# One step of a dense graph attention: the score products move from behind the transposes to the end of the step

## The chip, the core and the metric

The kernel runs on one core of one Trainium2 chip, as one launch. TensorE (PE) does the products and the transposes, VectorE (DVE) and ScalarE (ACT) the elementwise work, GpSimd (POOL) small parts, and SyncE (SP) issues most of the transfers. The metric is the device time of one execution in microseconds (us). Three timed runs of the kernel before gave 3488.07, 3489.20 and 3493.47 us, median 3489.2 us.

## The reference, cut to what matters

Four graph layers follow one another on 3125 nodes, 256 features and 100,000 edges, each with a residual and a layer norm behind it. The change touches only the first, an attention with 4 heads of 64 features:

```python
q = jnp.einsum('nd,hdk->nhk', x, Wq) + bq
k = jnp.einsum('nd,hdk->nhk', x, Wk) + bk
v = jnp.einsum('nd,hdk->nhk', x, Wv) + bv
scores = jnp.sum(q[dst] * k[src], axis=-1) / np.sqrt(HEAD_DIM).astype(np.float32)
seg_max = jax.ops.segment_max(scores, dst, num_segments=N)
ex = jnp.exp(scores - seg_max[dst])
denom = jax.ops.segment_sum(ex, dst, num_segments=N)
alpha = ex / (denom[dst] + 1e-16)
agg = jax.ops.segment_sum(alpha[:, :, None] * v[src], dst, num_segments=N)
out_h = agg + jnp.einsum('nd,hdk->nhk', x, Wskip) + bskip
```

The kernel does it densely. It counts the edges of every pair of nodes once, and each attention is then a softmax over a whole row of 3200 source nodes (25 tiles of 128), with the logarithm of the edge count added to the score; pairs without an edge get a huge negative number.

## The kernel before, in words

**The parts of the program.** They run one after the other: the edge counts and the projections, the first attention (names a_p_s, a_p_t, a_p_o; about 542 to 1580 us of the profile), the second attention by the same function `attend` with `dot=False` (to about 2470 us), and the sums with the last attention.

**The unit.** The first attention goes through 25 tiles of 128 target nodes times 4 heads, 100 units. A unit passes through these steps:

1. Scores (`score_part`, L1132): the 128 x 3200 scores are made in 8 pieces of 400 columns, each of two matmuls with the full 128 x 128 array (from sh_kt and sh_q) into one of two banks a_p_s. DVE adds the masks, takes the maximum and so frees the bank (`masked`, L1305; semaphore s_sfree), two pieces per slot.
2. ACT takes the exponential in place in a_sm (L1214; s_prob).
3. Transposes (`turn_block`, L1150): PE transposes the 25 blocks of a_sm in four slots of 7, 7, 7 and 4 blocks (`DOT_TURNS`, L805) into the two banks a_p_t, and ACT copies each slot back into a_sm (L1220; s_copy).
4. Weighing (`weigh`, L1173): 25 matmuls of the values a_v (64 columns) with the transposed rows. Block a writes partitions 0 to 63 or 64 to 127 of a_p_o, by whether a is even or odd (`r = (a % 2) * HD`), and the 25 blocks add up there. The profile shows each of these matmuls as two instructions, so 7 blocks are x14.
5. ACT copies the sums into a_sumT (`flip`, L1227; s_flip), PE turns them back (`turn_back`, L1180), and ACT scales them (L1239).

**The order.** It is written out by hand, engine by engine. In the loop step of unit n, PE transposes unit n, weighs unit n-1, makes the scores of unit n+2 and turns back unit n-2, slot by slot (u = 0 to 3). The steps for the layer's output (`posts`, names a_pp) come at the end of slots 1 and 3. With T, W and S for the transposes, the weighing and the scores of a slot, the order of the first attention is T0 S0 W0, W1 T1 S1, T2 S2 W2, W3 T3 S3, turn back. In the second attention there are no scores, and the order is T0 W0, T1 W1, T2 W2, T3 W3, with 8, 8, 8 and 1 blocks.

**The waits around it on PE.** A score piece waits until the piece two before it is masked, and the first score piece of a tile for its loads. T of a slot waits for the exponential of its columns and for the copy of the transposes two slots before. W0 waits for the flip of unit n-2, which ACT does at the start of the same step, behind the scaling of that unit; that scaling waits for the turn back at the end of the step before.

Of the kernel before, what the change touches and what calls it, by code (L numbers as in the profile page):

```python
# [808 lines left out]
def attend(nc, name, ident, dot, heads, passes, v_dram, post, full_dram, shared, log_dram=None, q_dram=None, kt_dram=None, al_src_dram=None, al_dst_dram=None, ct_dram=None, r2_dram=None):  # L809

    ctx = ExitStack()
    with ctx:
# [63 lines left out]
        def loaded(j):  # L876

            return 144 * (j // 2) + (128 if j % 2 else 0)
# [6 lines left out]
        def unit(p, j, par, half, h):  # L885

            t, gp, gh = tile_of(p, j, par, half)
            return t * heads + h, h if heads == 4 else 2 * gp + h

        def exists(at):  # L890

            return at is not None and not (isinstance(at[1], int) and at[1] >= NT)

        def following(at):

            p, j, par, half, h = at
            if h + 1 < heads:
                return p, j, par, half, h + 1
            if isinstance(j, int) and j == NT - 1 and p < final:
                return p + 1, 0, 0, 0, 0  # L900
            return p, j + 1, 1 - par, (half + 1 if par == 1 else half), 0
# [10 lines left out]
        def ahead(at, k):  # L912
            for _ in range(k):
                at = following(at)
            return at if exists(at) else None

        def behind(at, k):
            for _ in range(k):
                at = preceding(at) if at is not None else None
            return at if exists(at) else None  # L920
# [9 lines left out]
        def early(n, k):  # L930
            return isinstance(n, int) and n < k

        def units_loop(eng, body):

            for p in range(passes):
                tile_run(lambda j, par, half, first=False, last=False: [body((p, j, par, half, h)) for h in range(heads)])
            for k in range(P_.LAGS):
                for h in range(heads):
                    body((final, NT + k, (NT + k) % 2, (NT + k) // 2, h))

        def posts(eng, fn, at, u):

            p, j, par, half, h = at
            if p == final:
                for step in lagged(j, par, half):
                    fn(eng, h * ntu + u, *step)

        def score_bank(n, i):

            if n >= len(first_units):  # L950
                return p_s[i % 2][:, 0:SW]
            pair = (n * SU + i) // 2 % RING
            o = (i % 2) * UNIT
            return p_s[i % 2][:, 0:SW] if pair == 0 else p_t[pair - 1][:, o:o + SW]
# [4 lines left out]
        with nc.Block() as block:  # L959
# [154 lines left out]
            @block.tensor  # L1114
            def _(pe):
                def score_part(at, k, m):

                    p, j, par, half, h = at
                    n, buf = unit(*at)
                    if k == 0 and m == 0:  # L1120
                        if n == 0:
                            pe.wait_ge(shared.s_q, 128)
                        elif h == 0:
                            pe.wait_ge(s_in[par], loaded(j))
                        if n < heads:
                            pe.wait_ge(shared.s_kt[h], 96 if h < 2 else 32)
                    r, l = divmod(m, 2)
                    i = 2 * k + r
                    freed = n * SU + i - (1 if n >= len(first_units) else 2 * RING - 1)
                    if l == 0 and freed >= 1:  # L1130
                        pe.wait_ge(s_sfree, freed)
                    t = nc.tensor.matmul(score_bank(n, i), q[par][:, h, l, :], shared.keys(h)[:, i * SW:(i + 1) * SW], start=l == 0, stop=l == 1)  # L1132
                    if l == 1:
                        t.then_inc(s_s, 1)

                def turn_block(at, u, i):

                    n, buf = unit(*at)
                    if i == 0:
                        if u == 0 or e_part[u] != e_part[u - 1]:  # L1140
                            pe.wait_ge(s_prob, n * NE + e_part[u] + 1)
                        if dot and n == 0 and u == 0:
                            pe.wait_ge(s_sfree, len(first_units) * SU)
                        done = n * ntu + u - 1
                        if not early(done, 1):
                            pe.wait_ge(s_copy, done)
                        if u == 1 and not early(n, 3):
                            pe.wait_ge(s_norm, n - 2)
                    a = a_row[u] + i
                    m = nc.tensor.transpose(p_t[u % 2][:, i * P:(i + 1) * P], sm[buf][:, a * P:(a + 1) * P], ident[:, :])  # L1150
                    if i == turns[u] - 1:
                        m.then_inc(s_t, 1)

                def turn_and_score(at, u):

                    later = ahead(at, 2) if dot else None
                    for i in range(turns[u] if exists(at) else 0):
                        turn_block(at, u, i)
                    for m in range(0 if later is None else SCORE_PARTS):
                        score_part(later, u, m)  # L1160

                def weigh(at, u):

                    n, buf = unit(*at)
                    p, h = at[0], at[4]
                    if u == 0 and not early(n, 1):
                        pe.wait_ge(s_flip, n)
                    if early(n, 1) and u == 0:
                        pe.wait_ge(s_v, 16 if dot else 48)
                    pe.wait_ge(s_copy, n * ntu + u + 1)  # L1170
                    for a in range(a_row[u], a_row[u + 1]):
                        r = (a % 2) * HD
                        m = nc.tensor.matmul(p_o[r:r + HD, 0:P], v[:, a, (p * heads + h) * HD:(p * heads + h + 1) * HD], sm[buf][:, a * P:(a + 1) * P],  # L1173
                                             start=a < 2, stop=a >= NT - 2)
                    m.then_inc(s_pv, 1)

                def turn_back(at):
                    n, buf = unit(*at)
                    pe.wait_ge(s_flip, n + 1)
                    nc.tensor.matmul(back, sumT[:, at[4] % 2, :], twice[:, :], start=True, stop=True).then_inc(s_back, 1)  # L1180

                def body(at):
                    for u in range(ntu):
                        turns_first = not dot or u % 2 == 0
                        if turns_first:
                            turn_and_score(at, u)
                        if behind(at, 1) is not None:
                            weigh(behind(at, 1), u)
                        if not turns_first:
                            turn_and_score(at, u)  # L1190
                        if u == back_slot and behind(at, 2) is not None:
                            turn_back(behind(at, 2))
                        posts(pe, P_.pe, at, u)
                    if not dot and at[0] == 0 and at[4] == 0:
                        P_.pe_heavy(pe, at[1])
                    if isinstance(at[1], int) and at == first_tile_end:
                        P_.pe_init(pe)

                pe.wait_ge(s_const, 3)
                if dot:  # L1200
                    for at in first_units:
                        for k in range(SU // 2):
                            for m in range(SCORE_PARTS):
                                score_part(at, k, m)
                units_loop(pe, body)

            @block.scalar
# [196 lines left out]
SCORE_PARTS = 4  # L1404
# [600 lines left out]
class Tail:  # L2005
# [314 lines left out]
    def turn(self, pe, j, u):  # L2320

        if u == 0 or self.e_part[u] != self.e_part[u - 1]:
            pe.wait_ge(self.s_prob, j * NE + self.e_part[u] + 1)
        n = j * len(TURNS) + u
        if n >= 2:
            pe.wait_ge(self.s_copy, n - 1)
        for i in range(TURNS[u]):
            a = self.a_row[u] + i
            m = self.nc.tensor.transpose(self.p_t[u % 2][:, i * P:(i + 1) * P], self.sm[j % 2][:, a * P:(a + 1) * P], self.ident[:, :])  # L2329
        m.then_inc(self.s_t, 1)  # L2330
# [341 lines left out]
```

## Time and profile before

| what | value |
| --- | --- |
| timed runs, median of 3 | 3489.2 us |
| profiled execution, whole time | 3502.71 us |
| its span | 3501.0 us |
| PE busy | 3303.7 us (94%) |
| DVE busy | 2600.1 us (74%) |
| ACT busy | 2083.2 us (60%) |
| mean granted clock of TensorE | 0.984 of 2.4 GHz |

The profile is one execution. Busy time is time in which at least one instruction of an engine was under way; matmuls overlap, so the mean duration of one (some 280 ns for a 128-column matmul) says less than the distance from one to the next. A timeline row merges the instructions of one line: its first number is the start, the second its length, then the engine, the line, the operation, the output and inputs, and after x how many there are. In square brackets stands how long the engine had been idle just before and what ended that.

### The profile page before, as it was taken

What the parts mean: (1) busy time and instruction counts of PE and PEld (TensorE: products, weight loads), DVE (VectorE), ACT (ScalarE), POOL (GpSimd) and SP (SyncE); (2) the same over time, 40 slices, a digit from 0 to 9 for tenths busy, and PEclk for the clock granted to TensorE, in tenths of its full rate; (3) what the DMA queues carried; (4) which work ended last, traced back from release to release, by engine and by line L of the source; (5) the groups of instructions that cost most, each with busy time, mean ns of one, the idle gap of its engine ahead of it and who ended that gap; (6) DMA issues with size and microseconds to landing.
All of it is one profiled execution on the core that took longest, in us unless ns stands there. A gap on an engine that the chain in (4) does not pass through costs nothing. (4 is left out here: it accounts for less than half of the span.)

```text
span 3501.0 us, 67240 instructions
## 1 busy us (share of the span) xinstructions
PE 3303.7 (94%) x25814; PEld 2685.9 (77%) x25815; DVE 2600.1 (74%) x4799; ACT 2083.2 (60%) x3840; POOL 647.3 (18%) x604
## 2 busy tenths in 40 slices
PE   5999997999999999997999999999899999999998
PEld 3555556888888888885777777777688888878887
DVE  7899986766766766658999999999698443235665
ACT  2556555777766766776999999999211111115554
POOL 1010000111111111111255146666100000000000
PEclk9999998999999999998999999999999999999999
DMA  2565667333333433346333523333665555553341
GB/s 75 229 235 208 238 236 215 103 118 120 107 106 114 125 107 105 111 142 160 104 116 118 193 92 132 106 132 102 226 221 208 210 204 192 217 208 129 136 148 58
DMA packets 202699, 534.72 MB, mean 153 GB/s; under 512 B 56881, under 2 KB 165462, under 8 KB 168502
## 3 DMA queue, kind: packets, MB, share of 16 engines
q1 hardware_dynamic: 199494, 526.25, 43.5%
q10 hardware_dynamic: 1904, 3.81, 0.4%
q8 instruction: 191, 3.13, 0.4%
q0 software_dynamic: 1024, 0.82, 0.1%
q14 instruction: 86, 0.70, 0.1%
HBM read 362.87 MB, written 167.80 MB: 152 GB/s over the span
## 5 line engine op out<-in xcount | busy, mean ns | idle before, releaser
L1220 ACT ACTIVATE a_sm<-a_p_t 128x896 f32<-128x896 f32 (+3 forms) x800 | 670.5, 838 | 292.6 <-PE a_p_t L1150 235.3
L1150 PE MATMUL a_p_t<-ident,a_sm 128*128 128x128 f32 x5000 | 709.8, 279 | 34.7 <-ACT a_sm L1220 20.2
L1214 ACT ACTIVATE a_sm<-a_sm,a_negm 128x896 f32<-128x896 f32 (+3 forms) x600 | 702.7, 1171 | 48.5 <-DVE a_negm L1277 48.1
L1173 PE MATMUL a_p_o<-a_sm,a_v 128*64 128x128 f32 x10000 | 706.0, 280 | 21.4 <-ACT a_sumT L1227 19.2
L1173 PEld LDWEIGHTS a_p_o<-a_sm,a_v 128*64 128x64 f32 x10000 | 560.8, 138 | 142.5 <-issue 88.2
L1150 PEld LDWEIGHTS a_p_t<-ident,a_sm 128*128 128x128 f32 x5000 | 558.1, 142 | 135.0 <-issue 115.4
L1305 DVE CUSTOM_DVE_ANT_0 a_sm<-a_p_s,sh_rows 128x400 f32<-128x400 f32 x790 | 421.9, 571 | 308.5 <-PE a_p_s L1132 267.4
L1132 PE MATMUL a_p_s<-sh_kt,sh_q 128*128 128x400 f32 x1580 | 395.4, 371 | 36.5 <-DVE a_mx L1305 17.5
L1326 DVE SCALAR_TENSOR_TENSOR a_sm<-sh_wide,sh_al 128x3125 f32<-128x3125 f32 x100 | 346.9, 3469 | 3.6 <-PEq L54 1.8
L1336 DVE CUSTOM_DVE_ANT_0 a_sm<-a_sm,sh_rows 128x3125 f32<-128x3125 f32 x100 | 348.1, 3481 | 1.3 <-issue 0.3
L1132 PEld LDWEIGHTS a_p_s<-sh_kt,sh_q 128*128 128x128 f32 x1580 | 263.0, 191 | 49.8 <-DVE a_mx L1305 27.0
L2344 PE MATMUL t_acc<-t_v,t_sm 128*128 128x256 f32 x1250 | 287.5, 381 | 0.0
L583 DVE TENSOR_TENSOR hot_k<-iota_w,key_g 128x2400 bf16<-128x2400 f16 x200 | 279.7, 1399 | 0.0
L738 ACT ACTIVATE sh_wide<-p_g 128x400 f32<-128x400 f32 x200 | 149.3, 904 | 207.4 <-PE p_g L653 207.4
L2344 PEld LDWEIGHTS t_acc<-t_v,t_sm 128*128 128x128 f32 x1250 | 230.4, 191 | 31.9
L651 PE MATMUL p_g<-hot_k,hot_b 128*128 128x400 bf16 x1200 | 228.7, 340 | 21.0 <-DVE hot_k L583 20.3
L2228 PE MATMUL t_acc<-sh_messages,sh_ct 128*128 128x512 f32 x825 | 221.9, 410 | 9.9 <-PEq L54 9.2
L651 PEld LDWEIGHTS p_g<-hot_k,hot_b 128*128 128x128 bf16 x1200 | 113.7, 98 | 120.9 <-DVE hot_k L583 37.0
L2375 ACT ACTIVATE t_hT<-t_pp 128x256 f32<-128x256 f32 x50 | 19.3, 385 | 279.5 <-PE t_pp L2280 279.5
L2228 PEld LDWEIGHTS t_acc<-sh_messages,sh_ct 128*128 128x128 f32 x825 | 152.3, 190 | 39.9 <-issue 9.6
L2405 ACT ACTIVATE t_sm<-t_p_t 128x1024 f32<-128x1024 f32 x100 | 83.5, 835 | 165.3 <-PE t_p_t L2329 165.3
L2184 POOL TENSOR_SCALAR t_n_ve<-t_n_mv 128x1 f32<-128x1 f32 x50 | 10.9, 219 | 739.1 <-DVE t_n_mv L2583 531.8
(319 smaller groups left out, 4859.8 us busy)
## 6 DMA issues: line engine op xcount, KB each, us to landing
sh_rows<-d_full SPq DMA_DIRECT2D x67, 1600.0 KB, 7.1
sh_ct<-d_ct SPq DMA_DIRECT2D x50, 1600.0 KB, 6.7
d_ct<-sh_wide SPq DMA_DIRECT2D x25, 1600.0 KB, 5.3
d_full<-sh_rows SPq DMA_DIRECT2D x25, 1600.0 KB, 5.9
t_third<-d_ct SPq DMA_DIRECT2D x25, 1600.0 KB, 6.7
d_logs<-sh_rows SPq DMA_DIRECT2D x23, 1664.0 KB, 6.0
sh_rows<-d_logs SPq DMA_DIRECT2D x23, 1664.0 KB
sh_q<-d_q SPq DMA_DIRECT2D x200, 64.0 KB, 2.3
```

The source lines that it names most:

```text
L583: v.tensor_tensor(hot_k[k][:, q, :, :, :], iota_w[:, :, :].unsqueeze(1).to_broadcast([P, TRIP // 2, GW, 2]), by_two(key_g[k][:, q, :], GW) ...
L651: last = nc.tensor.matmul(p_g[:, q, 0:GW], hot_b[k][:, q, u // 2, :, u % 2], hot_k[k][:, q, u // 2, :, u % 2], start=False, stop=u == TRIP ...
L1132: t = nc.tensor.matmul(score_bank(n, i), q[par][:, h, l, :], shared.keys(h)[:, i * SW:(i + 1) * SW], start=l == 0, stop=l == 1)
L1150: m = nc.tensor.transpose(p_t[u % 2][:, i * P:(i + 1) * P], sm[buf][:, a * P:(a + 1) * P], ident[:, :])
L1173: m = nc.tensor.matmul(p_o[r:r + HD, 0:P], v[:, a, (p * heads + h) * HD:(p * heads + h + 1) * HD], sm[buf][:, a * P:(a + 1) * P], start=a ...
L1214: nc.scalar.activation(sm[buf][:, c], sm[buf][:, c], ACT.Exp, bias=negm[:, buf:buf + 1], accum_out=parts[:, buf, e:e + 1]).then_inc(s_prob, 1)
L1220: nc.scalar.activation(sm[buf][:, a_row[u] * P:a_row[u + 1] * P], p_t[u % 2][:, 0:turns[u] * P], ACT.Copy).then_inc(s_copy, 1)
L1305: v_.tensor_tensor_reduce(out=sm[buf][:, c], in0=score_bank(n, i), in1=full[par][:, c], scale=1.0, scalar=-3.0e38, op0=ALU.add, op1=ALU.ma ...
L1326: v_.scalar_tensor_tensor(sm[buf][:, 0:N], a_bc[:, h, 0, 0:N], al[gp][:, g:g + 1], a_bc[:, h, 1, 0:N], ALU.add, ALU.max).then_inc(s_lift, 1)
L1336: v_.tensor_tensor_reduce(out=sm[buf][:, 0:N], in0=sm[buf][:, 0:N], in1=mask[gp][:, 0:N], scale=1.0, scalar=-3.0e38, op0=ALU.add, op1=ALU. ...
L2228: m = self.nc.tensor.matmul(self.acc[t % 2][:, :], self.ct[t % 3][:, a * P:(a + 1) * P], self.messages[k % 2][:, a, :], start=a == 0, stop ...
L2344: m = self.nc.tensor.matmul(self.acc[t % 2][:, 0:D], self.sm[j % 2][:, a * P:(a + 1) * P], self.v3[:, a, :], start=a == 0, stop=a == NT - 1)
```

## The change

In each slot the scores of unit n+2 are made last, after both the transposes and the weighing. Nothing changes in slots 1 and 3, where they were last already. In slots 0 and 2 the order goes from T S W to T W S. Only PE's order changes, and only in the first attention. Every instruction, every buffer and every wait is as before.

```diff
-                def turn_and_score(at, u):
+                def score_ahead(at, u):
 
                     later = ahead(at, 2) if dot else None
+                    for m in range(0 if later is None else SCORE_PARTS):
+                        score_part(later, u, m)
+
+                def turn(at, u):
+
                     for i in range(turns[u] if exists(at) else 0):
                         turn_block(at, u, i)
-                    for m in range(0 if later is None else SCORE_PARTS):
-                        score_part(later, u, m)
...
                         turns_first = not dot or u % 2 == 0
                         if turns_first:
-                            turn_and_score(at, u)
+                            turn(at, u)
                         if behind(at, 1) is not None:
                             weigh(behind(at, 1), u)
                         if not turns_first:
-                            turn_and_score(at, u)
+                            turn(at, u)
+                        score_ahead(at, u)
                         if u == back_slot and behind(at, 2) is not None:
                             turn_back(behind(at, 2))
```

PE's queue in one unit of the first attention, from T0 to S1, before. The transposes (L1150) are followed by the scores (L1132), and W0 and W1 (L1173) stand together as 14 blocks:

```order
L1150 MATMUL a_p_t<-ident,a_sm 128x128 x7
L1132 MATMUL a_p_s<-sh_kt,sh_q 128x400 x4
L1173 MATMUL a_p_o<-a_sm,a_v 64x128 x14
L1150 MATMUL a_p_t<-ident,a_sm 128x128 x7
L1132 MATMUL a_p_s<-sh_kt,sh_q 128x400 x4
```

The same place of the changed kernel, where the weighing is L1176:

```order
L1150 MATMUL a_p_t<-ident,a_sm 128x128 x7
L1176 MATMUL a_p_o<-a_sm,a_v 64x128 x7
L1132 MATMUL a_p_s<-sh_kt,sh_q 128x400 x4
L1176 MATMUL a_p_o<-a_sm,a_v 64x128 x7
L1150 MATMUL a_p_t<-ident,a_sm 128x128 x7
L1132 MATMUL a_p_s<-sh_kt,sh_q 128x400 x4
```

The one run of 14 blocks has become two of 7, with the scores between them.

PE's queue from T2 to S3 before, where W2 and W3 stand together as 11 blocks:

```order
L1150 MATMUL a_p_t<-ident,a_sm 128x128 x7
L1132 MATMUL a_p_s<-sh_kt,sh_q 128x400 x4
L1173 MATMUL a_p_o<-a_sm,a_v 64x128 x11
L1150 MATMUL a_p_t<-ident,a_sm 128x128 x4
L1132 MATMUL a_p_s<-sh_kt,sh_q 128x400 x4
```

The same place of the changed kernel:

```order
L1150 MATMUL a_p_t<-ident,a_sm 128x128 x7
L1176 MATMUL a_p_o<-a_sm,a_v 64x128 x7
L1132 MATMUL a_p_s<-sh_kt,sh_q 128x400 x4
L1176 MATMUL a_p_o<-a_sm,a_v 64x128 x4
L1150 MATMUL a_p_t<-ident,a_sm 128x128 x4
L1132 MATMUL a_p_s<-sh_kt,sh_q 128x400 x4
```

Here the run of 11 has become one of 7 and one of 4. In the whole program PE's queue grows from 3398 such rows to 3592, two more in each of 97 units: the first unit has nothing to weigh, and the last two make no scores.

## Rows read from the trace of the kernel before

**Rows 1.** Windows: length, then busy us (count) of PE, PEld, DVE, ACT, POOL; PEclk, DMA share, GB/s.
```profile
570.00:1560.00 990.00, 967.13 (x9291) 858.23 (x9289) 679.36 (x2194) 718.07 (x1294) 137.16 (x208) 0.99 0.36 113
```

**Rows 2.** Groups by line, 560 to 1560 us: busy us, mean ns, idle before by releaser.
```profile
L1132 PE MATMUL a_p_s<-sh_kt,sh_q 128*128 128x400 f32 x1555 | 388.1, 371 | 22.2 <-DVE a_mx L1305 16.9 <-DMA sh_kt<-d_kt 5.3
...
L1173 PE MATMUL a_p_o<-a_sm,a_v 128*64 128x128 f32 x4866 | 324.7, 280 | 5.3 <-ACT a_sumT L1227 3.2 <-issue 2.1
```

**Rows 3.** Waits, 560 to 1560 us: total us, times, longest.
```profile
PE a_p_s L1132 <- DVE a_mx L1305: 16.9, 10, 3.2
...
PE a_p_o L1173 <- ACT a_sumT L1227: 3.2, 12, 0.3
```

**Rows 4.** Timeline of PE, first attention, W2 and W3 up to S1 of the next unit.
```profile
621.40 1.52 PE L1173 MATMUL a_p_o<-a_sm,a_v 128*64 128x128 f32 x22
622.86 0.65 PE L1150 MATMUL a_p_t<-ident,a_sm 128*128 128x128 f32 x4
623.27 0.98 PE L1132 MATMUL a_p_s<-sh_kt,sh_q 128*128 128x400 f32 x4
624.08 0.33 PE L1180 MATMUL a_p_t<-a_twice,a_sumT 128*128 128x64 f32 x2
624.25 0.94 PE L1150 MATMUL a_p_t<-ident,a_sm 128*128 128x128 f32 x7
624.94 0.98 PE L1132 MATMUL a_p_s<-sh_kt,sh_q 128*128 128x400 f32 x4
625.85 1.75 PE L1173 MATMUL a_p_o<-a_sm,a_v 128*64 128x128 f32 x28
627.53 0.98 PE L1150 MATMUL a_p_t<-ident,a_sm 128*128 128x128 f32 x7
628.27 0.98 PE L1132 MATMUL a_p_s<-sh_kt,sh_q 128*128 128x400 f32 x4
```

**Rows 5.** Timeline of PE, second attention, W3 of one block up to T1.
```profile
1999.98 0.43 PE L1173 MATMUL a_p_o<-a_sm,a_v 128*64 128x128 f32 x2
2000.34 0.43 PE L1180 MATMUL a_p_t<-a_twice,a_sumT 128*128 128x64 f32 x2
2000.61 1.04 PE L1150 MATMUL a_p_t<-ident,a_sm 128*128 128x128 f32 x8
2001.58 1.09 PE L1173 MATMUL a_p_o<-a_sm,a_v 128*64 128x128 f32 x16
2002.61 1.10 PE L1150 MATMUL a_p_t<-ident,a_sm 128*128 128x128 f32 x8
```

**Rows 6.** Timeline of all engines, PE's weight loads (PEld) into and out of a weighing.
```profile
1004.63 1.28 PEld L1173 LDWEIGHTS a_p_o<-a_sm,a_v 128*64 128x64 f32 x22 [0.27 <-issue]
...
1006.08 0.42 PEld L1150 LDWEIGHTS a_p_t<-ident,a_sm 128*128 128x128 f32 x4 [0.17 <-issue]
```

**Rows 7.** Timeline of PE, two of the ten waits for the masking, and what follows.
```profile
982.65 1.70 PE L1132 MATMUL a_p_s<-sh_kt,sh_q 128*128 128x400 f32 x4 [3.20 <-DVE a_mx L1305]
984.28 2.20 PE L1173 MATMUL a_p_o<-a_sm,a_v 128*64 128x128 f32 x22
...
1484.88 0.64 PE L1132 MATMUL a_p_s<-sh_kt,sh_q 128*128 128x400 f32 x2 [1.85 <-DVE a_mx L1305]
1485.44 1.52 PE L1173 MATMUL a_p_o<-a_sm,a_v 128*64 128x128 f32 x22
```

**Rows 8.** Timelines of ACT and PE: a usual flip, then a late one.
```profile
1007.95 0.27 ACT L1227 ACTIVATE a_sumT<-a_p_o 128x128 f32<-128x128 f32 x1
...
1007.48 0.94 PE L1150 MATMUL a_p_t<-ident,a_sm 128*128 128x128 f32 x7
...
705.23 0.32 ACT L1227 ACTIVATE a_sumT<-a_p_o 128x128 f32<-128x128 f32 x1
...
703.67 0.93 PE L1150 MATMUL a_p_t<-ident,a_sm 128*128 128x128 f32 x7
...
705.60 1.75 PE L1173 MATMUL a_p_o<-a_sm,a_v 128*64 128x128 f32 x28 [0.27 <-ACT a_sumT L1227]
```

## The prediction, made before the changed kernel was run

> **What bounds the kernel now.** I read the profile from the stage down to single products. First the windows: from 570 to 1560 us, nearly all of the first attention, PE is busy for 967 of 990 us at a granted clock of 0.99, while DVE is busy for 679 and ACT for 718 [rows 1]. So PE sets the time there, and what the change adds to PE's own sequence lands on the span, since the next stage begins when this one is done. Then the groups and the waits: all that PE loses to others in this stretch is 16.9 us of score products waiting for DVE's masking, 10 times, 3.2 us of weighing waiting for ACT's flip, 12 times, and 5.3 us once for a load of the keys [rows 2, 3]. A better order of the same instructions has at most these some 25 us to win. Last the timeline of one quiet unit, which shows what PE's sequence costs without any wait, from the start of one block to the start of the next [rows 4]: 7 transposes 0.69 us after the turn back and 0.74 after a weighing, scores 0.81 before the turn back and 0.91 before a weighing, a weighing of 14 blocks (x28) 1.68, one of 11 blocks (x22) 1.46.
>
> **What a run of weighing costs.** This decides the case. Even and odd blocks go to different halves of the array. If the two halves work side by side, one pair of blocks (four instructions) is two passes of time, and a block without a partner takes two passes as well. The rows say so. 14 blocks are 7 pairs, 14 passes: 1.68 us. 11 blocks are 5 pairs and one alone, 12 passes: 1.46 us. The difference of 0.22 for two passes is 0.11 per pass, and it leaves 1.68 - 14 x 0.11 = 0.14, with the unrounded pass of 0.109 some 0.15 per run, whatever its length. In the second attention 8 blocks are 8 passes, which gives 1.02 and reads 1.03, and a single block is 2 passes, 0.37, and reads 0.36 [rows 5]. A rule of one pass per block without the rounding up would give the single block 0.26 and the 11 blocks 1.35, which the rows refuse. Beside the 0.15 per run there is the way in: scores take 0.91 before a weighing and 0.81 before a full-width product [rows 4], 0.10 more. In both places PE's weight loads stand still for no other engine, 0.27 us on the way in and 0.17 on the way out [rows 6].
>
> **The change, first place (T0 to T1).** Before: T0 0.69 + S0 0.91 + W0 and W1 1.68 = 3.28 us [rows 4]. After, T0 leads into a weighing: the second attention shows 8 transposes after a turn back into a weighing at 0.97 [rows 5], and one transpose is (0.74 - 0.41) / 3 = 0.11 [rows 4], so 0.86. W0 has 7 blocks, 3 pairs and one alone, 8 passes like the run of 8: 1.03. S0 now begins in an array that has just left a weighing. No row shows scores behind a weighing. From below it is the 0.91 of scores behind transposes. From above it is 0.96, since transposes lose 0.05 there (0.74 against 0.69). The nearest row is a half of scores that began after a wait: 0.56 us to the weighing [rows 7], where half of the usual four products, (0.91 - 0.18) / 2 + 0.18 by their spacing of 0.18 us (0.91 for four and one more spacing), makes 0.545, so 0.015 more. I take 0.93. W1 has 7 blocks, again 8 passes: 1.03. Sum 0.86 + 1.03 + 0.93 + 1.03 = 3.85, so +0.57 us.
>
> **Second place (T2 to T3).** Before: 0.69 + 0.91 + 1.46 = 3.06. After: T2 0.86, W2 of 7 blocks 1.03, S2 0.93, W3 of 4 blocks, 4 passes, 0.15 + 4 x 0.11 = 0.59. Sum 3.41, so +0.35 us. There is no added lone block here, because 11 blocks had one already.
>
> Together 0.92 us per unit, of which 0.22 is the lone block of the first place and the rest four more changes between half and full width. Times 97 units: **+89 us**. The eight rounded terms may be off by 0.04 us a unit, 4 us in all.
>
> **What hides it.** Nothing that I find: no other engine is near its bound in this stage, and a unit only becomes longer, so DVE, ACT and the loads get more time, not less.
>
> **Waits that change.** (a) W0 loses the cover of S0 while it waits for the flip. In the usual unit the flip ends at 1007.95 + 0.27 = 1008.22, and with T0 at 1007.48 the weighing could now begin at 1007.48 + 0.86 = 1008.34; a flip reaches it some 0.05 us after its end (705.55 to 705.60) [rows 8]. That leaves 0.07 us, which is enough but thin. In the late case the flip ends at 705.55, and T0 began at 703.67, so W0 could begin at 704.53 and waits until 705.60, about 1.07 us, where it waits about 0.3 now. For 12 such units [rows 3] that is at most 12 x 0.75 = +9 us. But between T2 and T3 ACT now has 0.35 us more to catch up, so I take **+5 us**. Below: 0. (b) The scores' waits for the masking [rows 3]. The large ones stand in front of S2 or in its middle, where DVE has been held up itself. The run W2 can now be done within the wait, up to 1.02 us of each. Taken over the ten this is about 7 us, and after a wait of 3.20 us the granted clock was at 1.2 GHz for a while, the x22 run lasting 2.20 instead of 1.52 [rows 7]; a shorter wait may save one or two of these. Also the second score run no longer follows the first so closely (S1 to S2 gains W2's time). I take **-9 us**; from above 0, from below all 16.9 and some 5 of clock, -22.
>
> Sum: 89 + 5 - 9 = +85 us. The profiled execution, 3502.7 us whole (its span is 3501.0), becomes 3588. It lies 13.5 us above the median of the runs; the timed median goes from 3489.2 to **3574 us**, 2.4% slower.
>
> The Trainium skill, in TensorEngine Tiling (Array Packing), Key Properties, says that "Changing tiling mode (not just tile) drains the TensorE"; it gives no price. The 0.15 per run and the idle weight loads of rows 6 agree with it. It is the rule that speaks against this change, since it makes each of the four new changes of width cost something, W to S too.
>
> **The rivals.**
> 1. *Scores follow a weighing for free.* The run's 0.15 is read only where transposes or the turn back follow it; if the scores' products could be loaded behind a weighing as they are behind transposes, 2 x 0.15 and 2 x 0.02 per unit fall away, 0.34 x 97 = 33 us: +52, 3541 us. Against it: transposes too are full width, and their loads stand idle for 0.17 [rows 6]. The Trainium skill, TensorE: Matmul & The Clock Gate, on the engine's queue depths, has a reorder window that pulls weight loads ahead of running matmuls; by it alone this rival would be right, and rows 6 shows that the window does not reach over a change of width. Chance 0.13.
> 2. *The flip's cover goes everywhere.* The margin of 0.07 us is gone if ACT is a little later in the usual unit, as when a copy of 0.6 us comes before the scaling. If half of the 97 units then wait 0.5 us: +24, 3598 us. For it: the 12 late units, and that the second attention, which has this order, waits for the same flip. Against it: units with a post product between turn back and T0 have 0.2 us more. Chance 0.10.
> 3. *Faster, because the masking is what holds PE.* With the scores at even distances, DVE never holds a bank, the 16.9 us and the slow clock behind them go (-22), and the mode changes cost nothing, because the half-width passes are only the spacing of a busy queue: 3467 us. It wins over the cost only if a unit grows by less than 22 / 97 = 0.23 us. The single block of rows 5, 0.36 us for one product, alone speaks against it. Chance 0.03.
> 4. *No change*: the added time lies where PE would have waited anyway. PE's idle time of about 23 us in 990 [rows 1] has no room for 89. Chance 0.02.
> 5. *The lone block is not paid* (it overlaps the scores' first load): 0.22 x 97 = 21 us less, 3553 us. Against it: 11 blocks, with a lone last one, pay their 12th pass before transposes. Chance 0.10.
>
> The forecast of 3574 has the remaining 0.62. A measurement of this kernel can tell about 0.2%, 7 us, from no change; faster than that 0.03, within it 0.02, slower 0.95. The range goes from 3535 us (rival 1 with all that the waits could give beyond the 9 taken for a part of it) to 3600 us (rival 2).
>
> **What the profile of the changed kernel would show.** From T0 to T1 of a quiet unit 3.85 us, from T2 to T3 3.41, with W0, W1 and W2 each as x14 and 1.03 us to the next block, and W3 as x8 and 0.59. The first attention ends about 85 us later, and the second attention has its old length. Weight loads of the scores idle for about 0.2 us behind each weighing; if they don't, it is rival 1. The flip's waits remain about 12 but near 1 us, and many more would be rival 2. Score waits for the masking drop below 10 us. The forecast is wrong if T0 to T1 takes under 3.5 us, or if PE's idle time in this stage grows by more than 20 us.

## The result, and the profile after

| | before | changed |
| --- | --- | --- |
| timed runs, median | 3491.3 us (4 runs) | 3564.4 us (4 runs, 3560.6 to 3567.1) |
| profiled execution, whole | 3502.7 us | 3562.8 us |
| its span | 3501.0 us | 3561.1 us |

The changed kernel is slower by 73 us: ratio 1.0198, interval 1.0179 to 1.0217. The forecast was +85 us, to 3574 us with a range of 3535 to 3600.

The place first. The view of one line's instructions gives, for each kind, the count, the shortest, median and longest duration in ns, and the start of the first and the last one in us. The score products of before, then of the changed kernel:

```profile
L1132 PE MATMUL a_p_s<-sh_kt,sh_q x1580: 337/346/702, 541.7 to 1557.7; 128*128 128x400 f32 x198
```
```profile
L1132 PE MATMUL a_p_s<-sh_kt,sh_q x1580: 337/345/702, 541.7 to 1618.4; 128*128 128x400 f32 x198
```

The first score starts at the same time in both, the last one 60.7 us later, and the span grew by 60.1. All the time was lost in the first attention, and nearly nothing (0.6 us) was given back behind it. The profiled execution of before lay 11 us above the median of its runs and that of the changed kernel 2 us below, so the two profiles differ by 60 and the medians by 73.

The timeline of PE for a quiet unit of the changed kernel, from T0 to the T1 after it and on to the next unit (W is L1176 here, the turn back L1183):

```profile
640.03 0.93 PE L1150 MATMUL a_p_t<-ident,a_sm 128*128 128x128 f32 x7
640.88 1.09 PE L1176 MATMUL a_p_o<-a_sm,a_v 128*64 128x128 f32 x14
641.90 1.00 PE L1132 MATMUL a_p_s<-sh_kt,sh_q 128*128 128x400 f32 x4
642.83 1.09 PE L1176 MATMUL a_p_o<-a_sm,a_v 128*64 128x128 f32 x14
643.85 0.98 PE L1150 MATMUL a_p_t<-ident,a_sm 128*128 128x128 f32 x7
...
645.40 0.93 PE L1150 MATMUL a_p_t<-ident,a_sm 128*128 128x128 f32 x7
646.26 1.09 PE L1176 MATMUL a_p_o<-a_sm,a_v 128*64 128x128 f32 x14
647.28 0.99 PE L1132 MATMUL a_p_s<-sh_kt,sh_q 128*128 128x400 f32 x4
648.20 0.66 PE L1176 MATMUL a_p_o<-a_sm,a_v 128*64 128x128 f32 x8
648.79 0.65 PE L1150 MATMUL a_p_t<-ident,a_sm 128*128 128x128 f32 x4
```

Read the starts. T0 to T1 is 643.85 - 640.03 = 3.82 us, where it was 3.28 [rows 4]. T2 to T3 is 648.79 - 645.40 = 3.39, where it was 712.10 - 709.05 = 3.05 by the timeline of PE before:

```profile
709.05 0.93 PE L1150 MATMUL a_p_t<-ident,a_sm 128*128 128x128 f32 x7
...
712.10 0.65 PE L1150 MATMUL a_p_t<-ident,a_sm 128*128 128x128 f32 x4
```

The terms are 0.85 and 0.86 for the transposes, 1.02 for each run of 7 blocks, 0.93 and 0.92 for the scores, and 0.59 for the run of 4.

The whole units show where the time went. The distance from one T0 to the next was read for the 95 units behind 577 us and sorted by the head that is being transposed. The mean of each kind, in us:

| head of the tile | before | changed | difference |
| --- | --- | --- | --- |
| first (24 units) | 9.26 | 10.15 | +0.89 |
| second (23) | 9.62 | 10.38 | +0.76 |
| third (24) | 11.44 | 11.40 | -0.04 |
| fourth (24) | 10.53 | 11.44 | +0.91 |

The other heads also hold products for the layer's output, and nearly all the stalls. The first heads are the quiet ones: they differ by less than 0.03 us among themselves in either kernel, and they grew by 0.89 us. 97 such units would be +86 us. The third heads did not grow at all, so there some 22 us of stalls of before are missing.

PE's weight loads in another quiet stretch of the changed kernel:

```profile
652.06 0.67 PEld L1132 LDWEIGHTS a_p_s<-sh_kt,sh_q 128*128 128x128 f32 x4 [0.17 <-issue]
652.99 0.85 PEld L1176 LDWEIGHTS a_p_o<-a_sm,a_v 128*64 128x64 f32 x14 [0.26 <-issue]
654.01 0.75 PEld L1150 LDWEIGHTS a_p_t<-ident,a_sm 128*128 128x128 f32 x7 [0.17 <-issue]
654.73 0.67 PEld L1132 LDWEIGHTS a_p_s<-sh_kt,sh_q 128*128 128x128 f32 x4
```

The first row is what no row of before could show: scores behind a weighing. Their load stands still for 0.17 us, as that of transposes behind a weighing does [rows 6]. Behind transposes (the last row) it does not.

The waits of the changed kernel from 560 to 1635 us, in total, times, longest:

```profile
PE a_p_s L1132 <- DVE a_mx L1309: 6.2, 8, 2.5
PE a_p_o L1176 <- ACT a_sumT L1231: 4.7, 10, 1.0
```

The waits for the masking fell from 16.9 to 6.2 us, and those for the flip rose from 3.2 to 4.7 [rows 3]. These rows count only idle time in front of a product. They explain 9 us of the 26 between 86 and 60; the other 17 us do not stand in these two rows. In the third heads of before, blocks from T2 to the turn back were longer than in quiet units also where no idle time stands in front of them: W2 and W3 together, for one, took 1.73 us in the mean and not 1.46. The slowed x22 of [rows 7] is such a case.

### The profile page after: what moved, and what is told of

Its sections match the earlier page's. It is cut to its first block and busy times, and to the rows that moved or that the text cites. A ratio compares the mean times of both kernels' runs of the same rounds, so it can differ in the third digit from the quotient of the medians.

```text
span 3561.1 us, 67240 instructions
## 1 busy us (share of the span) xinstructions
PE 3380.4 (95%) x25814; PEld 2706.3 (76%) x25815; DVE 2602.9 (73%) x4799; ACT 2084.5 (59%) x3840; POOL 648.1 (18%) x604
## 5 line engine op out<-in xcount | busy, mean ns | idle before, releaser
L1176 PE MATMUL a_p_o<-a_sm,a_v 128*64 128x128 f32 x10000 | 764.9, 281 | 24.1 <-ACT a_sumT L1231 19.3
L1150 PE MATMUL a_p_t<-ident,a_sm 128*128 128x128 f32 x5000 | 712.1, 280 | 33.0 <-ACT a_sm L1224 19.2
L1176 PEld LDWEIGHTS a_p_o<-a_sm,a_v 128*64 128x64 f32 x10000 | 573.2, 137 | 176.2 <-issue 111.1
L1150 PEld LDWEIGHTS a_p_t<-ident,a_sm 128*128 128x128 f32 x5000 | 560.2, 143 | 133.1 <-issue 113.4
L1132 PE MATMUL a_p_s<-sh_kt,sh_q 128*128 128x400 f32 x1580 | 394.9, 372 | 20.2 <-DVE a_twice L1372 13.8
L1132 PEld LDWEIGHTS a_p_s<-sh_kt,sh_q 128*128 128x128 f32 x1580 | 264.1, 190 | 59.1 <-issue 33.5
L2348 PEld LDWEIGHTS t_acc<-t_v,t_sm 128*128 128x128 f32 x1250 | 230.0, 190 | 31.7
L1493 POOL TENSOR_SCALAR a_n_ve<-a_n_mv 128x1 f32<-128x1 f32 x50 | 11.1, 222 | 785.8 <-DVE a_n_mv L1488 785.8
```

What stands on the lines that cost most here:

```text
L2348: m = self.nc.tensor.matmul(self.acc[t % 2][:, 0:D], self.sm[j % 2][:, a * P:(a + 1) * P], self.v3[:, a, :], start=a == 0, stop=a == NT - 1)
```

## The experiments

Eight kernels ran in two groups of four, each group on one chip with its own runs of before, and a ninth by itself. All ratios are against the kernel before of the same group. The diffs show the changed lines with a few around them.

**The changed kernel again** (no edit).

> The changed kernel itself beside the three others, on the same chip: +73 us against before by every theory, as the measure for the others.

Measured: 3577.3 us, 1.0216 (1.019 to 1.0242) against 3499.3, so +78 us. Its last score starts at 1631.8 us, 13 us later than in the first profile of the same kernel. Executions of one kernel on one chip spread as much: before's seven in this group lie between 3491.1 and 3508.4 us. The first, second and fourth heads last as long as in the first profile, within 0.04 us; the third heads last 11.88 us in the mean and not 11.40, which is 11 of the 13 us. What follows about 10 us or less rests on the rows and not on the medians.

**Slot 0 alone, slot 2 alone.** The edit against the changed kernel. k is the slot that keeps the order of before, so it is 2 for slot 0 alone and 0 for slot 2 alone:

```diff
+                        early_scores = u == k
                         if turns_first:
                             turn(at, u)
+                        if early_scores:
+                            score_ahead(at, u)
                         if behind(at, 1) is not None:
                             weigh(behind(at, 1), u)
                         if not turns_first:
                             turn(at, u)
-                        score_ahead(at, u)
+                        if not early_scores:
+                            score_ahead(at, u)
```

> The scores move behind the weighing in slot 0 only; slot 2 keeps the order of before. Theory (each extra run of weighing pays two changes of array width, and an odd run a lone block): slot 0 adds 3.83 - 3.28 = 0.55 us per unit, 53 us in 97 units, less some 5 to 10 us of waits that shrink: +43 to +53 us against before. T0 to T1 takes 3.83 us, T2 to T3 the old 3.05. Rival (the cost is not in the runs but in the scores coming later for VectorE, the same in both slots): about half of the whole, +36 us. Rival (the waits shrink only when both slots are even): +53 or more.

> The scores move behind the weighing in slot 2 only. Theory: slot 2 adds 3.39 - 3.05 = 0.34 us per unit (no new lone block, since the run of 11 had one), 33 us in 97 units, less the waits for the masking, which stand in front of the scores of slot 2: +18 to +33 us against before, clearly less than slot 0 alone. Rival (scores later, the same in both slots): +36 us. The sum of this one and of slot 0 alone should be the whole change, +73 us, within 10 us.

Measured: slot 0 alone 1.0174 (1.014 to 1.0208), +57 us; slot 2 alone 1.0106 (1.0082 to 1.013), +36 us. Slot 0 costs 21 us more, as the lone block demands (0.22 x 97). Slot 2 alone came out where the rival also put it, at +36 us, so it decides nothing between the two; slot 0 alone does, since its interval (+49 to +73 us) excludes the rival's +36. Each is a little over its range, and together they make 94 us, not 78. The sum missed its 10 us, though the intervals of the three ratios leave some 17 us open. The timeline of PE with slot 0 alone, in the first head of a tile, shows a reason in slot 0:

```profile
643.55 0.93 PE L1150 MATMUL a_p_t<-ident,a_sm 128*128 128x128 f32 x7
644.63 1.12 PE L1132 MATMUL a_p_s<-sh_kt,sh_q 128*128 128x400 f32 x4
645.68 1.52 PE L1176 MATMUL a_p_o<-a_sm,a_v 128*64 128x128 f32 x22
```

T2 to S2 takes 1.08 us where a head without the wait takes 0.68 (the same kernel, 653.92 and 654.60), and S2 to W2 1.05 instead of 0.91. That is 0.55 us more, in the unit in which DVE also masks a quarter of the tile's rows in every slot. S0 has become later while S2 still follows S1 closely, so DVE has not freed the banks. PE's weight loads waited 65 times for the masking there, with 31.7 us in all, against 37 times before. In the changed kernel W2 stands in that gap and the wait is gone:

```profile
PEld a_p_s L1132 <- DVE a_mx L1305: 24.9, 37, 3.5
```
```profile
PEld a_p_s L1132 <- DVE a_mx L1313: 31.7, 65, 3.2
```
```profile
PEld a_p_s L1132 <- DVE a_mx L1309: 10.3, 19, 2.9
```

The first row is of before (560 to 1560 us), the second of slot 0 alone (560 to 1625 us), the third of the changed kernel (560 to 1635 us). So the two moves are not independent: the second one hides a wait that the first one makes. From T2 to W2 it stands in 22 of the 24 first heads, 12 us in all. That would be most of the 16 us that the sum is off by. For slot 2 alone the 3 us over the range are within the spread.

**The old order, made longer by repeated transposes.** The edit is against before. The quiet unit becomes as long as the changed kernel's, 10.14 us from T0 to T0.

```diff
                     for i in range(turns[u] if exists(at) else 0):
+                        if later is not None and i == turns[u] - 1:
+                            for k in range({0: 5, 2: 3}.get(u, 0)):
+                                nc.tensor.transpose(p_t[u % 2][:, k * P:(k + 1) * P], sm[unit(*at)[1]][:, (a_row[u] + k) * P:(a_row[u] + k + 1) * P], ident[:, :])
                         turn_block(at, u, i)
```

> The order of before, but TensorE transposes five blocks a second time in slot 0 and three in slot 2 (8 x 0.109 = 0.87 us more per unit, as much as the change adds), in all units that make scores. It asks why the change cost 73 us and not the 86 that 97 units of 0.89 us make. Theory A (a longer unit alone gives VectorE and ScalarE time, so that their waits and the slow clock behind them shrink): the same as the changed kernel, +65 to +80 us. Theory B (it is the order that shrinks them, the weighing being done inside the wait and the scores standing at more even distances): the waits for the masking stay near 17 us, and it is +85 to +90 us.

Measured: 1.0223 (1.0198 to 1.0248), +77 us, against 1.0216 for the changed kernel in the same group. The same length in the old order costs the same. That is theory A, though the interval (+69 to +87 us) does not exclude the +85 of theory B. The waits are smaller too, where theory B left them near 17 us:

```profile
PE a_p_s L1132 <- DVE a_mx L1308: 8.9, 9, 2.2
```

(560 to 1640 us). That the products done inside a wait shorten it, which the prediction counted on, is not needed for the gain. But how much of the fall from 16.9 us a longer unit causes is not shown: the kernel with even slots in the old order, below, has units as short as before and also waits 8.9 us in its profile. The flip's waits are 1.0 us here and 4.7 in the changed kernel; that difference would be the price of the lost cover, from one profile of each.

**Weighing at full width, in either order.** A block is multiplied with two heads' values at once, onto all 128 partitions, so that no product of the weighing is half width. The same lines go into before and into the changed kernel:

```diff
+                        if dot:
+                            g = min(h, 2) * HD
+                            m = nc.tensor.matmul(p_o[:, 0:P], v[:, a, g:g + 2 * HD], sm[buf][:, a * P:(a + 1) * P], start=a == 0, stop=a == NT - 1)
+                            continue
```

> The order of before, with the weighing made full width: each block is one product of 128 value columns onto all 128 partitions (two heads' values instead of one, so the sums are not the layer's). Every block now costs two passes of 0.11 us and no change of width remains. Theory: per unit 25 x 0.22 = 5.5 us of weighing instead of 14 + 12 passes and two runs' 0.15 and entries of 0.1 (3.3 us), so about +2.2 us x 99 = +215 us against before. It is the base for the next.

> The changed order with the same full-width weighing (the sums are again not the layer's). Theory (the change costs only through changes of array width and the lone block): no cost is left, so it is within 7 us of the full-width kernel in the old order, and W0 to S0 shows no idle weight load. Rival (the cost lies in the order of the scores, in the flip's lost cover or in VectorE's waits): still some +50 to +85 us over the full-width kernel in the old order.

Measured: 3673.7 us in the old order (1.0547, 1.0529 to 1.0564) and 3678.1 in the new one (1.0558, 1.054 to 1.0575). The base came out at +189 us and not +215. The quiet unit grew from 9.26 to 11.39 us, 211 us for 99 units, and nearly all stalls had vanished (PE waited 0.2 us for the masking). The order then makes 4 us, within the intervals. So without half-width runs the order costs nothing that can be measured. As the stalls are gone in both full-width kernels, this pair cannot say what the flip's lost cover or the masking contribute at half width; that they are small rests on the wait rows and on the repeated transposes. The weighing pays both for changes of width and for the lone block, and the next pair separates the two. The weight loads of the new order at full width:

```profile
644.08 0.80 PEld L1150 LDWEIGHTS a_p_t<-ident,a_sm 128*128 128x128 f32 x7
644.85 1.64 PEld L1178 LDWEIGHTS a_p_o<-a_sm,a_v 128*128 128x128 f32 x14
646.41 0.67 PEld L1132 LDWEIGHTS a_p_s<-sh_kt,sh_q 128*128 128x128 f32 x4
```

No load stands idle into or out of the weighing.

**Slots with even numbers of blocks, in either order.** Again the same lines go into before and into the changed kernel.

```diff
-DOT_TURNS = [7, 7, 7, 4]
-DOT_EXPS = [0, 7 * P, 14 * P, NPAD]
+DOT_TURNS = [8, 6, 8, 3]
+DOT_EXPS = [0, 8 * P, 14 * P, NPAD]
```

> The order of before with slots of 8, 6, 8 and 3 blocks instead of 7, 7, 7 and 4; the exponential's parts are cut at 8 and 14 blocks. Runs of weighing stay 14 and 11 blocks. By every theory nothing on TensorE changes: within 7 us of before. It is the base for the next.

> The changed order with slots of 8, 6, 8 and 3 blocks. W0 has 8 blocks and W1 6, so that no run but W3 has a lone block, and W3 had it before. Theory (a lone block costs two passes, 0.22 us): 0.22 x 97 = 21 us less than the changed kernel: +52 us against before, with T0 to T1 at 3.6 us instead of 3.83. Rival (the lone block is not the cost, the runs' changes are all of it): no difference to the changed kernel, +73 us.

Measured: in the old order 0.9994 (0.998 to 1.0008), no difference. Its profile has these waits for the masking (560 to 1560 us), half of before's 16.9 at the same length of unit, and its 95 units together are 20 us shorter, 14 of them in the third heads:

```profile
PE a_p_s L1132 <- DVE a_mx L1305: 8.9, 5, 3.0
```

In the new order 1.0165 (1.0148 to 1.0182), +58 us, some 15 to 20 us under the changed kernel. The interval, +52 to +63 us, excludes the rival's +73. The timeline of PE in the new order with these slots, from T0 to T1:

```profile
648.34 1.04 PE L1150 MATMUL a_p_t<-ident,a_sm 128*128 128x128 f32 x8
649.31 1.09 PE L1176 MATMUL a_p_o<-a_sm,a_v 128*64 128x128 f32 x16
650.34 0.99 PE L1132 MATMUL a_p_s<-sh_kt,sh_q 128*128 128x400 f32 x4
651.25 0.88 PE L1176 MATMUL a_p_o<-a_sm,a_v 128*64 128x128 f32 x12
652.06 0.88 PE L1150 MATMUL a_p_t<-ident,a_sm 128*128 128x128 f32 x6
```

The run of 6 blocks takes 652.06 - 651.25 = 0.81 us, that of 8 takes 1.03, and that of 7 took 1.02 above. A run of 7 costs what a run of 8 does. T0 to T1 is 3.72 us here with one transpose more in T0 (0.11), which makes 3.61 for comparison, 0.21 less than with 7 and 7. That is the lone block by itself.

**All 25 blocks in one run.** The edit is against the changed kernel.

```diff
                         turns_first = not dot or u % 2 == 0
-                        if turns_first:
+                        if dot:
+                            if u == 2 and behind(at, 1) is not None:
+                                for k in range(ntu):
+                                    weigh(behind(at, 1), k)
+                            turn(at, u)
+                        else:
                             turn(at, u)
-                        if behind(at, 1) is not None:
-                            weigh(behind(at, 1), u)
-                        if not turns_first:
-                            turn(at, u)
+                            if behind(at, 1) is not None:
+                                weigh(behind(at, 1), u)
                         score_ahead(at, u)
```

> All 25 blocks of a unit are weighed in one run, before T2: T0 S0, T1 S1, W0 to W3, T2 S2, T3 S3, turn back. Theory: if each run of weighing pays about 0.15 us on the way out, 0.10 on the way in and 0.05 behind it, one run instead of two saves 0.30 us per unit, at the same 26 passes (13 pairs), 99 x 0.30 = 30 us less on TensorE. But the four score slots now stand 1.3 to 1.7 us apart with the long run only once between them, and VectorE's masking takes 1.07 us per slot, 2.1 and more in a tile's first head; I expect waits of 0.3 to 1 us in one unit of four, +8 to +24 us. Together -22 to -5 us against before. Rival (the masking's waits take all of it): 0 to +10 us.

Measured: 3517.4 against 3485.9 us, 1.0096 (1.0076 to 1.0117), so about +33 us. Both the theory's sum and the rival missed. The run itself costs what the model says, and the rest of the unit shows what went wrong (timeline of PE):

```profile
712.36 0.60 PE L1150 MATMUL a_p_t<-ident,a_sm 128*128 128x128 f32 x4
712.84 1.13 PE L1132 MATMUL a_p_s<-sh_kt,sh_q 128*128 128x400 f32 x4
713.80 0.33 PE L1183 MATMUL a_p_t<-a_twice,a_sumT 128*128 128x64 f32 x2
714.51 1.13 PE L1630 MATMUL a_pp<-a_wout,a_oT 128*128 128x256 f32 x4 [0.38 <-ACT a_oT L1687]
...
718.61 3.05 PE L1176 MATMUL a_p_o<-a_sm,a_v 128*64 128x128 f32 x50
721.60 0.98 PE L1150 MATMUL a_p_t<-ident,a_sm 128*128 128x128 f32 x7
```

25 blocks are 13 pairs, 26 passes: 26 x 0.109 + 0.15 = 2.98, and 2.99 is read. But T3 and S3 together take 713.80 - 712.36 = 1.44 us, where they took 1.22 [rows 4], because S3 comes only 1.3 us after S2 and waits for a bank, and not in one unit of four but in nearly each (PE's weight loads waited 169 times for the masking, 39.4 us in all). The post product of the layer's output, once per tile, also waits now for the copy by ACT in front of it, since the weighing that used to stand between T2 and the turn back has gone (turn back to product 0.71 us where 0.17 is usual; 9.6 us in 24 waits). So the score distances that I took to matter little do matter when they fall under DVE's time. The version does not help.

No version beats the kernel before; the even slots in the old order equal it.

## Why the prediction was right, point by point

- *PE sets the time of the first attention, and what its sequence gains in length lands on the span.* Right: the last score moved by 60.7 us and the span by 60.1, and a unit made longer by transposes alone cost the same as the change (+77 and +78 us). It holds for the added length; the stalls of the stage fell at the same time, so less than the 86 us arrived.
- *A run costs 0.11 us per pass, two passes per pair or lone block, and 0.15 besides.* Right, for 25, 8, 7, 6 and 4 blocks: 2.99, 1.03, 1.02, 0.81 and 0.59 us. The even slots showed the lone block by itself, 0.21 us per unit in the rows.
- *Scores behind a weighing, 0.93 us, the one term without a row.* Measured 0.93 and 0.92. The run before them takes 1.02, with the same 0.15 at its end. Rival 1, for free, is out, and so is rival 5. The Trainium skill, TensorEngine Tiling (Array Packing), Key Properties, has the rule that a change of tiling mode drains TensorE, which the prediction weighed. The traces agree with it: at full width the idle loads are gone and the order costs 4 us.
- *+89 us for 97 units.* 3.82 - 3.28 and 3.39 - 3.05 give 0.54 + 0.34 = 0.88 us per unit, and the quiet first heads give 0.89, 86 us. The prediction's 0.92 carried 0.03 of rounding: eight terms, read at 0.01 and mostly rounded up.
- *Flip +5 us.* It was mis-sized: 3.2 to 4.7 us is +1.5, in 10 waits of 0.5 us in the mean and not near 1. That ACT had caught up more than I allowed is the likely reason; no run isolates it. The usual unit kept its thin margin, as rows of the changed kernel show for a usual and a late flip:

```profile
650.65 0.27 ACT L1231 ACTIVATE a_sumT<-a_p_o 128x128 f32<-128x128 f32 x1
...
651.05 1.09 PE L1176 MATMUL a_p_o<-a_sm,a_v 128*64 128x128 f32 x14
...
802.18 0.32 ACT L1231 ACTIVATE a_sumT<-a_p_o 128x128 f32<-128x128 f32 x1
...
802.55 1.09 PE L1176 MATMUL a_p_o<-a_sm,a_v 128*64 128x128 f32 x14 [0.56 <-ACT a_sumT L1231]
```

  In the first, the flip ends at 650.92 and W0 starts at 651.05, 0.13 later, so it did not wait. In the second it starts 0.05 after the flip. Rival 2 is out.
- *Waits for the masking -9 us.* The idle rows say -10.7 us, but the agreement is partly luck. The stalls of the whole stage fell by 26 us between the first two profiles, and two profiles of one kernel, the changed one, differ by 13 us through them. The even slots in the old order show 8.9 us of masking waits where before shows 16.9. Of the reasons given, W2 between S1 and S2 does hide a regular wait, the one that slot 0 alone showed; before did not have it. That the longer unit alone shortens the waits fits the repeated transposes, with the limit said there.
- *The sum.* 86 + 1.5 - 10.7 = 77 us by the idle rows, against medians of +73 and +78. This comparison mixes two things, since the rows come from the two profiles, and these differ by 60 us: there 86 - 26 = 60. With the medians, 86 + 1.5 leaves 10 to 15 us that the other stalls gave back, where the prediction had 9. Of the 12 us between forecast and result 3 are rounding and 4 the flip; the other 5 are stalls, and within the spread.
- *Rivals 3 and 4.* Rival 3, faster, needed a unit that grows by less than 0.23 us, and it grew by 0.89. Rival 4, no change, needed idle time for it, and the span grew by 60 us.

What stays open is why DVE and ACT now and then stand still together for up to 6 us in this stage, as they do in front of the wait of 3.20 us [rows 7], and how much of the time given back in the third heads the change itself causes. No experiment was made on either.

## What to carry to other kernels

Before moving work on a saturated TensorE, write its sequence as blocks with the distance from start to start for each pair of neighbours, and count how many times the array changes between half and full width: here each further run of half-width products cost about 0.34 us (3.39 - 3.05), and a lone block as much as a pair, 0.22 us. A more even spacing of products for a consumer is worth something only where that consumer is late; look at its waits first, here 17 us of waits in the profile of before against a cost of 86. And parts of such a change need not add up, since one part can hide a wait that another makes.

## What was not expected of the hardware

- Two executions of the same kernel had their last score product at 1618.4 and 1631.8 us, while quiet units repeat to 0.01 us. Nearly the whole spread, 11 of 13 us, is in the third heads of the tiles.
- A lone half-width block costs two full passes (0.22 us) even when products of full width follow at once.
- With weighing at full width the quiet unit is 2.13 us longer, 211 us for 99 units, and the kernel lost 189 us: with a longer unit nearly all stalls of the stage were gone.
